# A graph network in one launch: one operand of each two-input vector operation of the edge loops moved to PSUM

## What is computed

```python
# L0, twice (8 relations, 4 heads); L1 is the same with 1 relation and 1 head, and elu
alpha = leaky_relu(qn[etype, dst] + kn[etype, src], 0.2)
amax  = segment_max(alpha, dst)
ex    = exp(alpha - amax[dst])
agg   = segment_sum(ex[:, :, None] * xw[etype, src], dst) / segment_sum(ex, dst)
# L2 (8 relations): a weight for each edge
node  = segment_sum(xw[etypes, src] * norm, dst)
# L3: a message from both ends of an edge, scattered by src
msg   = relu(h[dst] + edge_feats);  red = segment_sum(msg, src)
# then a two-layer perceptron with a layer norm on h * (1 + eps) + red
```

## Time and profile before

| | |
|---|---|
| median of 3 runs | 29,700.3 us (29,672.3 to 29,722.3) |
| span of the profiled execution | 29,733.4 us |
| POOL busy | 21,017 us, 71% of the span |
| DVE busy | 10,285 us, 35% |
| PE, PE's weight loads, ACT busy | 2,997, 2,439, 960 us |
| DMA | 1,669 MB, mean 56 GB/s |

### The profile page before, as it was taken

The page is one execution under the profiler, slowest core; times in us unless marked ns, Lnnn a source line. Parts: engine busy times, 40 slices in busy tenths (PEclk is TensorE's granted clock), DMA queues, the critical chain, the costliest instruction groups (busy, mean ns, idle before and its releaser), DMA issues.

```text
span 29733.4 us, 103170 instructions
## 1 busy us (share of the span) xinstructions
PE 2997.2 (10%) x15266; PEld 2438.6 (8%) x15266; DVE 10285.3 (35%) x32260; ACT 959.9 (3%) x2365; POOL 21017.1 (71%) x17125
## 2 busy tenths in 40 slices
PE   2000000110000001000000211111111212212212
PEld 1000000000000000000000101011011212212212
DVE  2444444334444442222222233333333222222223
ACT  1000000000000000000000100000000000000000
POOL 6777777667777776777776555555556888888885
PEclk9999999999999999999999855555555555555555
DMA  4222222222222221111111211111112333333333
GB/s 165 78 74 72 79 78 73 79 75 57 55 58 56 58 53 42 48 43 45 48 43 47 72 38 37 35 38 37 35 38 56 48 43 49 48 43 49 48 43 62
DMA packets 1074924, 1668.82 MB, mean 56 GB/s; under 512 B 727554, under 2 KB 761518, under 8 KB 1024722
## 3 DMA queue, kind: packets, MB, share of 16 engines
q0 software_dynamic: 908672, 571.49, 15.2%
q1 hardware_dynamic: 114114, 928.44, 8.1%
q10 hardware_dynamic: 51728, 165.46, 1.6%
HBM read 948.27 MB, written 847.59 MB: 60 GB/s over the span
## 4 chain that ended last, share of the span: by engine, by line
issue 39%; DVE 22%; POOL 21%; another core or an unknown queue 11%; PE 5%; DMA 1%; ACT 1%; POOLq 0%; ACTq 0%; DVEq 0%; SPq 0%
POOL acc L592 11%; DVE region L1372 11%; POOL region L518 10%; PE ps L778 2%; DVE region L1129 2%; DVE region L1352 2%; DVE region L1342 2%; DVE region L1299 1%; PE ps L861 1%; DVE region L1365 1%; PE ps L833 1%; PE ps L835 1%; DVE region L1136 1%; DVE region L1312 1%
## 5 line engine op out<-in xcount | busy, mean ns | idle before, releaser
L518 POOL DMA_INDIRECT region<-table,idx x12896 | 14216.3, 1102 | 6630.3 <-issue 3911.2
L592 POOL DMA_INDIRECT acc<-region,idx x3224 | 5802.6, 1800 | 1018.9 <-issue 1003.3
L1372 DVE TENSOR_TENSOR_SCAN region<-region 128x62 f32<-128x62 f32 x9984 | 2881.8, 337 | 4171.6 <-issue 4157.9
L778 PE MATMUL ps<-ident,region 128*128 128x128 f32 x6448 | 1530.0, 386 | 9199.5 <-DVE region L1124 4324.3
L1352 DVE SCALAR_TENSOR_TENSOR region<-ps,region,lower 128x128 f32<-128x128 f32 x3224 | 993.9, 349 | 2701.3 <-remote 1366.1
L778 PEld LDWEIGHTS ps<-ident,region 128*128 128x128 f32 x6448 | 1096.5, 206 | 9508.8 <-issue 4096.5
L869 PE MATMUL ps<-ident,region 128*68 128x128 f32 (+1 forms) x3 | 1.3, 443 | 15107.4 <-DVE region L1392 15107.4
L1124 DVE CAST region<-src 128x62 f32 x52 | 10.1, 194 | 4197.1 <-POOLq L591 4084.8
L1323 DVE TENSOR_TENSOR region<-region 128x248 f32<-128x248 f32 (+1 forms) x156 | 77.3, 496 | 3742.3 <-DMA region<-table,idx 3720.7
L869 PEld LDWEIGHTS ps<-ident,region 128*68 128x68 f32 (+1 forms) x3 | 0.4, 150 | 15107.7 <-DVE region L1392 15107.7
L861 PE MATMUL ps<-region 128*128 128x64 f32 x6448 | 1035.0, 317 | 1148.8 <-ACT region L737 1148.8
(11 more groups left out here) (198 smaller groups left out, 4797.4 us busy)
## 6 DMA issues: line engine op xcount, KB each, us to landing
sums<-region SPq DMA_DIRECT2D x104, 2232.0 KB
region<-table,idx POOLq DMA_INDIRECT x12896
sums<-region SPq DMA_DIRECT2D x52, 2046.0 KB
region<-q_rel ACTq DMA_DIRECT2D x104, 992.0 KB
h_edge<-zeros_d SPq DMA_DIRECT2D x52, 1984.0 KB
sums<-region SPq DMA_DIRECT2D x52, 1984.0 KB
region<-h_edge SPq DMA_DIRECT2D x52, 1984.0 KB
region<-in_edge_attr SPq DMA_DIRECT2D x52, 1984.0 KB
```

Of the source, the lines that this page charges most:

```text
L518: pool.indirect_dma_start(out=to, out_offset=None, in_=table, in_offset=bass.IndirectOffsetOnAxis(ap=index, axis=0)).then_inc(s, 16)
L592: pool.indirect_dma_start(out=acc[BATCH * k + j % BATCH], out_offset=bass.IndirectOffsetOnAxis(ap=idx[:, b, j:j + 1], axis=0), in_=MSG[:, ...
L778: last = pe.transpose(ps[:, n % 2, c * P:(c + 1) * P], src_b[:, j:j + 1].to_broadcast([P, P]), ident[:, :])
L1372: last = dve.tensor_tensor_scan(O[:, b, :, f], fac_j, G[:, b, :, f], O[:, ob, J - 1, f:f + 1], ALU.mult, ALU.add)
```

## The change

The scans and the two-input element-wise operations of the edge loops get one of their inputs, or their output with it, from PSUM.

- `CJ[b]` (banks 4 and 5) is a copy of the chunk's piece of `cont`, which ACT makes for every chunk of every pass in the new `continued(i, b)`; DVE waits for it on `cj_in` at the start of a chunk and gives the buffer back on `cj_free` at its end. In RGCN ACT copies the edge weights for the chunk in the same way into `EWP[b]`.
- The one-hot `OH`, the scores `Q`, the leaky relu's result `LQ`, the differences `EX` and the flags `NEG` lie in banks 0 to 3, in GAT also the carried query `TM`. `NEGs` and `Qs` are copies of `NEG` and of the score that stay in SBUF, since the other input of their readers is in PSUM.
- ACT takes the exponentials from bank 3 to bank 6 (`EF`), and once more those that the denominators need straight into the columns of `G` that held the key term.
- The leaky relu is two instructions (a product, a maximum) in place of one; the two differences for `EX[:, 0]` are taken in the other order.

```diff
+        CJ = [bank(4 + b, 0, J) for b in range(2)]
+        EWP = [bank(4 + b, J, J) for b in range(2)]
...
+                def continued(i, b):
+                    at = i * (2 * J) + b * J
+                    act.wait_ge(cj_free, i * 2 + ((CH + 2) * l + b + 1))
+                    if l == RGCN:
+                        act.copy(EWP[b], cut(at_q, EPP)[:, bass.ds(at, J)])
+                    act.copy(CJ[b], cont[:, bass.ds(at, J)]).then_inc(cj_in, 1)
...
                         for b in range(2):
+                            continued(i, b)
                             act.wait_ge(e_free, i * 2 + ((CH + 2) * nth + b + 1))
...
-                            act.activation(ex, ex, ACT.Exp).then_inc(ex_out, 1)
+                            act.activation(G[:, b, :, D:D + h].rearrange("p j h -> p h j"), bank(3, h * J, h, J), ACT.Exp)
+                            act.activation(bank(6, 0, 2 * h * J), ex, ACT.Exp).then_inc(ex_out, 1)
...
-                        cj = cont[:, bass.ds(at, J)]
+                        cj = CJ[b]
...
+                        dve.wait_ge(cj_in, i * 2 + (CH * GINE + b + 1))
...
-                    TM = cut(at_q + 3 * w_e, J, k)
-                    OH = cut(at_s, J, REL)
-                    Q = cut(at_s + 500, h, J)
+                    TM = cut(at_q + 3 * w_e, J, k) if rels > 1 else bank(0, J, J, k)
+                    OH = bank(1, 0, J, REL)
+                    Q = bank(2, 0, h, J)
+                    EX = bank(3, 0, 2, h, J)
+                    EF = bank(6, 0, 2, h, J)
+                    LQ = bank(2, h * J, h, J)
+                    NEG = bank(0, 0, J)
+                    Qs = cut(at_s + 500, h, J)
...
+                            done(ts_(NEGs, cj, -1.0, BIG, ALU.add, ALU.mult))
...
-                            done(tt(Q, qv, G[:, b, :, D:ri].rearrange("p j h -> p h j"), ALU.add))
+                            done(tt(Qs, qv, G[:, b, :, D:ri].rearrange("p j h -> p h j"), ALU.add))
                             settle()
-                            done(stt(out=Q, in0=Q, scalar=SLOPE, in1=Q, op0=ALU.mult, op1=ALU.max))
+                            done(ts_(LQ, Qs, SLOPE, None, ALU.mult))
                             done(dve.tensor_copy(M[:, b, :, 0:1], M[:, ob, :, J:J + 1]))
                             settle()
+                            done(tt(LQ, LQ, Qs, ALU.max))
+                            settle()
...
-                                last = tt(gh[:, :, hh, :], gh[:, :, hh, :], bc(EX[:, 1, hh, :], 2, D // h), ALU.mult)
+                                last = tt(gh[:, :, hh, :], gh[:, :, hh, :], bc(EF[:, 1, hh, :], 2, D // h), ALU.mult)
...
-                            done(tt(g_b, g_b, bc(ew[:, bass.ds(at, J)], 2, D), ALU.mult))
+                            done(tt(g_b, g_b, bc(EWP[b], 2, D), ALU.mult))
...
-                            fac_j = EX[:, 0, f * h // D, :] if h else cj
+                            fac_j = EF[:, 0, f * h // D, :] if h else cj
```

More of the change, by code:

```diff
@@ L251, in build, with bank @@
         ps = ctx.enter_context(nc.psum_tensor("ps", [P, 8, 512], F32))
+        def bank(k, at, *shape):
+            v = ps[:, k, at:at + int(np.prod(shape))]
+            if len(shape) == 2:
+                v = v.rearrange("p (a b) -> p a b", a=shape[0])
+            elif len(shape) == 3:
+                v = v.rearrange("p (a b c) -> p a b c", a=shape[0], b=shape[1])
+            return v
+        CJ = [bank(4 + b, 0, J) for b in range(2)]
+        EWP = [bank(4 + b, J, J) for b in range(2)]
         zeroed = sem("zeroed")
@@ L302, in build @@
         chunk_begun = sem("chunk_begun")
+        cj_free = sem("cj_free")
+        cj_in = sem("cj_in")
         ew_free = sem("ew_free")
@@ L727, in _ @@
                     act.dma_start(cut(at_q, EPP), a["edge_weight1"].rearrange("(p j) k -> p (j k)", p=P)).then_inc(ew_in, 16)
+                    act.wait_ge(ew_in, 16)
+                    with act.Fori(0, CH // 2) as i:
+                        for b in range(2):
+                            continued(i, b)
                 if h:
@@ L1270, in _ @@
                 done(dve.memset(O[:, 1, J - 1, :], 0.0))
+                dve.sem_inc(cj_free, 2)
                 if h:
@@ L1275, in _ @@
                     QX = cut(at_q + 2 * w_e, J, k)
-                    TM = cut(at_q + 3 * w_e, J, k)
-                    OH = cut(at_s, J, REL)
-                    Q = cut(at_s + 500, h, J)
+                    TM = cut(at_q + 3 * w_e, J, k) if rels > 1 else bank(0, J, J, k)
[6 more added lines that the diff above has]
+                    Qs = cut(at_s + 500, h, J)
                     M = cut(at_s + 1500, 2, h, J + 1)
-                    EX = cut(at_s + 1000, 2, h, J)
-                    NEG = cut(at_s + 2010, J)
+                    NEGs = cut(at_s + 2010, J)
+                    iota_p = bank(1, J * REL, REL)
+                    done(dve.tensor_copy(iota_p, iota_r[:, :]))
                     done(dve.memset(M[:, 1, :, J:J + 1], -BIG))
@@ L1287, in _ @@
                     dve.wait_ge(ew_in, 16)
-                per = {CONV1: 24, CONV2: 24, GAT: 18, RGCN: 10}[l]
+                per = {CONV1: 28, CONV2: 28, GAT: 22, RGCN: 10}[l]
                 settle()
@@ L1292, in _ @@
                         at = i * (2 * J) + b * J
-                        cj = cont[:, bass.ds(at, J)]
+                        cj = CJ[b]
                         ob = 1 - b
+                        dve.wait_ge(cj_in, i * 2 + (CH * l + b + 1))
                         if h:
@@ L1333, in _ @@
                             settle()
-                            done(tt(EX[:, 0], M[:, b, :, 0:J], M[:, b, :, 1:J + 1], ALU.subtract))
+                            done(tt(EX[:, 0], M[:, b, :, 0:J], bc(NEG, 1, h), ALU.add))
                             settle()
-                            done(tt(EX[:, 0], EX[:, 0], bc(NEG, 1, h), ALU.add))
-                            tt(EX[:, 1], Q, M[:, b, :, 1:J + 1], ALU.subtract).then_inc(ex_in, 1)
+                            done(tt(EX[:, 0], EX[:, 0], M[:, b, :, 1:J + 1], ALU.subtract))
+                            tt(EX[:, 1], LQ, M[:, b, :, 1:J + 1], ALU.subtract).then_inc(ex_in, 1)
                             dve.wait_ge(ex_out, i * 2 + (CH * nth + b + 1))
```

14 lines of the change are left out of this document (8 added, 6 removed).

## The result

| | kernel before | changed | ratio, 95% interval |
|---|---|---|---|
| median of 4 runs each, us | 29,708.25 | 27,801.15 | 0.9362 [0.9349, 0.9375] |
| span of the profiled execution, us | 29,733.4 | 27,798.2 | |

The account below looks back on a forecast made before the run. Above POOL's floors lay POOL instructions stretched by DVE's SBUF scans and POOL's waits for row numbers. 29,733 - 604 + 0 - 385 + 0 + 100 = 28,844, as run median 28,810 us; own range 28,100 to 29,500, 8-in-10 range 26,100 to 29,800.

Parts of the forecast that it names:

- GINE, -604: GINE's 64 scans a chunk read flags from PSUM, so the scatter beside them takes 1.555, not 13.17 us: -604 us.
- GAT, -385: GAT's gather chunk falls from 92.4 to 85 us, chosen between floor and present: -385 us, bounds -770 and +437.
- RGCN, 0: RGCN's comparison is untouched and POOL is already idle when its multiplication and scans run: 0.
- Added work, +100: Extra copy, maximum, wait and second exponential: about 1 us a chunk in CONV1 and CONV2, +100 us.
- Operand price, 0: A scan with one input in PSUM costs no more than with both in SBUF: 0, bounds 0 to some 10 ns.
- CONV1 and CONV2, 0: Gathers are freed, but POOL then waits 20 us a chunk for late row numbers: sum 0, bounds -2,170 and +680.
- slow cadence: State in gather passes where each DVE instruction costs 1.40 us, 1.05 of it idle; set in 18 us after POOL's start.
- A: DVE's 1.05 us idle is waiting for POOL's access; PSUM inputs remove it, gather passes but RGCN reach floors: 26,160 us; 0.22.
- B: Slow cadence spreads in CONV1, CONV2 and GAT once POOL is no longer blocked: +609, or 30,300 us; chance 0.20.
- C: SBUF starting value or remaining SBUF tensor still keeps POOL out; nothing freed, only added 100 us: 29,800 us; chance 0.08.

Follow-up runs that it names:

- x1: Kernel before with only GINE's 64 scans a chunk reading the continuation flags from PSUM: 29,106 us against 29,743, ratio 0.9782.
- x3: Kernel before with only the factor of the sum and denominator scans in PSUM in CONV1, CONV2 and GAT: 28,775 us against 29,743, ratio 0.9673.
- x6: Changed kernel with 16 more one-column PSUM memsets a chunk in CONV1, CONV2 and GAT: 28,186 us; kernel before 29,743, ratio 0.9473.
- x8: Kernel before with the gather buffer handed back before the sum scans, operands still in SBUF: 28,723 us against 28,639, ratio 1.0028.
- a2: Changed kernel once more, on a chip without the slow cadence: 24,218 us; kernel before 28,692, ratio 0.8440.
- x9: Changed kernel with the gather buffer handed back before the sum scans, on a chip with the slow cadence: 28,711 us; kernel before 29,766, ratio 0.9638.
- x7: Changed kernel with the gather buffer handed back before the sum scans, on a chip without the slow cadence: 24,218 us; kernel before 28,639, ratio 0.8456.
- a1: Changed kernel once more, on another chip with the slow cadence: 27,882 us; kernel before 29,766, ratio 0.9367.
- x10: Changed kernel with each sum scan over only the second half of the columns, with the slow cadence: 27,645 us; kernel before 29,766, ratio 0.9289.

## Why the prediction was right and wrong

**GINE, -604: right.** -636 in the comparison, -637 on its own (x1). **GAT, -385:** -276. By the forecast's own measure (busy and idle time over the count, times 62) the chunk went from 92.4 to 87.2, where 85 was forecast; 85 was a value chosen between two bounds. **RGCN, 0:** -73, a chunk 1.4 us shorter, whose cause no run isolates. **Added work, +100:** no run isolates it either. **Operand price, 0: right.** GINE's scans took 320 ns with one input in PSUM in the changed kernel and 329 with both in SBUF in x3. The 58 and 120 cycles that the Trainium skill gives ("VectorE: DVE Perf Modes", section on the TRN2 errata), read as a price for the one input in PSUM, made +1,200, which was turned down on the earlier trace rows; these scans don't show it either.

**CONV1 and CONV2, 0: this step failed; it was -962.** Freeing POOL was right to the row (951 ns). What failed was the chunk laid out with RGCN as the model: slow cadence 18 us after POOL's restart, the head at its price (16.35 us), its end 9 us behind POOL's last gather, and so 98 us as before, with POOL's wait up to 20 us. Measured were 87.7 and 88.2 us a chunk and waits of 11.3 and 11.7. The changed kernel's chunk had the onset at 38.7 us and the head at 5.0, so that 19 sum scans were through when the slow cadence came, where the forecast had none. From the row-number copy at t = 0 POOL's last gather ended at 78.6 (forecast 78), the slow stretch at 83.8 (86), with 17 scans left (35), and the next copy came at 89.6 (98). Of these 8.4 us, 2.2 are the earlier end, 3.4 the shorter remainder (17 scans in 5.2 us, where 35 were put at 8.6), and 2.8 the last copy and its wait (0.6 where 3.4 were left for them). I took the onset from one chunk of RGCN, whose instructions are others (62 comparisons and 62 accumulator reads come first), and treated it as a constant. The direct evidence of the exchange rate was missed as well: in the kernel before, hold and wait add up to a chunk, and nothing in the rows made them trade one for one. In CONV1 x3 shows no trade at all for the first half of the hold, x3 and the changed kernel together some 60% for the second, x6 a growth of 3 us for sixteen instructions. That the trade comes from DVE's leftover running at the ordinary pace behind POOL's last gather fits all three and the timeline, but was not isolated by a run. Why the onset came at 33 to 39 us here and at 18 in RGCN stays open; that it did is what the traces show.

**The rivals.** A, the slow cadence as the port: refuted as a mechanism, since with PSUM inputs the sum scans still lost 5,555 us to it, and memsets without any input lost 1,207. On the chips without the cadence the outcome is like A's all the same, every pass on its floor, and by more than A's sum, since RGCN is there too. The Trainium skill's rule cited with A ("SBUF — State Buffer", "Who interferes with whom") holds for what it is about: two SBUF inputs held POOL 21.5 us a chunk (x8), one held it for nothing (a2). B, slower: the changed kernel didn't show it. x9 fits it, 830 us lost by letting POOL run beside more of DVE's chunk, with an edit that costs nothing where the cadence is absent (x7). C, nothing freed: excluded by the 951 ns.

**What stays open** is what the slow cadence is. It is per instruction, 1.40 us, independent of operands, length and bytes, seen beside POOL's gathers and for 5 to 9 us behind them, and on three of the five chips only. GINE's scans, beside POOL's scatters, don't show it: they stood idle for 7.8 us in all before 3,328 scans in the changed kernel. Two candidates aren't told apart by any run. One is the number of DMA packets, which no run lowers without lowering the number of gathers. The other is the recording of events: the Trainium skill, "NOTIFIC — the notification-queue block", section "Overflow: three behaviours, one of which stalls the engine", says that the internal pipeline of event records holds its producers up rather than lose a record. Nothing here shows that it does so in this case, and no run compares the kernel with and without such records.

## What to carry to other kernels

When DVE and POOL share a stretch, put one input of each two-input DVE instruction in PSUM; the gain is what POOL is held, less what DVE's remaining work lengthens POOL's wait, so split the idle time of POOL into held and waiting and price both. A stretch whose instructions start at a fixed distance whatever their size may come with the chip and not with the kernel: time the kernel before on several chips, and compare only within one. An edit that is free on one kind of chip (x7 beside a2) cost 3% on the other (x9 beside a1).

## What the runs showed of the hardware beyond the case

- The same kernel took 28,639 and 28,692 us on two chips and 29,743, 29,766 and 29,781 on three, and the changed kernel 24,218 and 27,882: 15% between chips. Some 3,100 of the 3,664 us between those two lie in the four gather passes (59.7 us over the four chunks, 52 times), where one trace has the slow cadence and the other has not; the rest lies outside them.
- On a chip with the cadence a memset of one column (59 ns) behind every fourth scan stood idle for 0.48 us before it on average; scans of 31 in place of 62 elements stood idle for 6,152 us (x10) in place of 5,582 (a1).
- GINE's 3,328 scans of 62 elements, one close behind the other, took 320 ns with one input in PSUM (321 in a1), and 329 with both in SBUF (x3).
- One DVE input in SBUF beside another in PSUM held no gather (mean 951 ns in all four passes of the changed kernel); two in SBUF, with POOL never waiting, brought CONV1's mean to 1,298 ns (x8).
